# Attention on rounded f32 halves with scores and maxima on separate row halves, and a last layer norm done batch by batch

## The reference, cut to what matters

```python
# attention: x [4096, 256], 16 heads of D = 16, K = 64
qh, kh, vh = heads(q @ in_proj_weight.T + in_proj_bias);  qh = qh / sqrt(d)
scores = einsum('bhid,bhjd->bhij', qh, kh)
rel    = clip(pos[None, :] - pos[:, None], -K, K) + K
bias   = take_along_axis(einsum('bhid,rd->bhir', qh, rel_pe), rel, axis=-1)
attn   = softmax(scores + bias, axis=-1)
x = layernorm(x + einsum('bhij,bhjd->bhid', attn, vh) @ out_w.T + out_b)
# two layers on x seen as (2, 2048, 256), 8 heads of 64
for l in range(2):
    h = shift_token(x)
    q, k, v = split(h @ wqkv[l])          # l2 norm, scale, rotation
    x = x + local_attention(q, k, v) @ wo[l]          # windows of 128, one back
    h = layernorm(shift_token(x)) * lg + lb
    a, g = split(h @ w1[l] + b1[l])
    x = x + (a * gelu(g)) @ w2[l] + b2[l]
x = layernorm(x_before_the_layers + x)
```

## Time and profile before

| | |
|---|---|
| median of 3 runs | 5778.08 us (5756.49 to 5778.12) |
| the profiled execution's own time | 5783.44 us |
| its span | 5781.8 us |
| PE busy | 5294.7 us (92%) |
| DVE busy | 4105.4 us (71%) |
| ACT busy | 3109.6 us (54%) |
| POOL busy | 953.5 us (16%) |

### The profile page before, as it was taken

One profiled execution on the slowest core, in us unless ns is written; L12 is line 12 of the kernel. 1 busy time (PEld: TensorE's weight loads), 2 busy tenths in 40 slices (PEclk: granted clock), 3 DMA queues, 4 the chain that ended last, 5 costly groups with the idle time before them and its releaser, 6 DMA issues. The chain is left out here.

```text
span 5781.8 us, 113252 instructions
## 1 busy us (share of the span) xinstructions
PE 5294.7 (92%) x33984; PEld 2681.2 (46%) x33984; DVE 4105.4 (71%) x8598; ACT 3109.6 (54%) x4537; POOL 953.5 (16%) x704
## 2 busy tenths in 40 slices
PE   7499999999999999999999999985999898999895
PEld 3233333333333333333333333332888654888653
DVE  4388888888888888888888888832777433777434
ACT  3256666666666666666666666630555312565310
POOL 0111111111111111111111111101333101333100
PEclk8589999999999999999999999975999899999997
DMA  6511112111111111112111111112000000000000
GB/s 166 141 40 53 48 54 56 48 53 54 50 53 53 48 54 55 48 53 54 50 53 53 47 52 47 52 43 91 1 0 0 16 0 16 1 0 0 30 0 29
DMA packets 203462, 254.49 MB, mean 44 GB/s; under 512 B 71086, under 2 KB 132852, under 8 KB 201588
## 3 DMA queue, kind: packets, MB, share of 16 engines
q1 hardware_dynamic: 199524, 232.98, 14.3%
q0 software_dynamic: 3856, 20.45, 1.3%
HBM read 210.73 MB, written 42.47 MB: 44 GB/s over the span
## 5 line engine op out<-in xcount | busy, mean ns | idle before, releaser
L745 DVE TENSOR_REDUCE group_max<-shared_ps 128x1 f32<-128x512 f32 x4096 | 2684.7, 688 | 586.7 <-PE shared_ps L469 484.2
L622 ACT ACTIVATE probs<-scores 128x1024 f32<-128x1024 f32 x2048 | 2012.3, 1021 | 1052.9 <-PE scores L495 673.7
L469 PE MATMUL shared_ps<-keys,max_queries 96*128 96x512 bf16 x4096 | 1436.1, 385 | 3.2 <-issue 1.7
L495 PE MATMUL scores<-queries,keys 98*128 98x512 bf16 (+3 forms) x4096 | 1218.5, 372 | 86.6 <-ACT probs L622 85.6
L510 PE MATMUL out_ps<-probs,values 128*17 128x512 f32 x8192 | 1089.2, 604 | 0.4 <-ACT probs L622 0.4
L469 PEld LDWEIGHTS shared_ps<-keys,max_queries 96*128 96x128 bf16 x4096 | 396.1, 97 | 1123.5 <-DVE group_max L745 507.9
L215 POOL TENSOR_TENSOR near_window<-near_bias,one_f 128x1536 bf16<-128x1536 f32 x128 | 351.5, 2746 | 2953.7 <-DVE max_parts L739 2305.8
L495 PEld LDWEIGHTS scores<-queries,keys 98*128 98x128 bf16 x4096 | 360.3, 98 | 465.7 <-ACT probs L622 236.9
L1303 PE MATMUL quad<-h_T,w 128*128 128x512 f32 (+1 forms) x768 | 344.3, 599 | 1.9 <-ACT h_T L1417 1.9
L521 PE MATMUL shared_ps<-block_q,block_table 96*128 96x32 bf16 x4096 | 271.5, 233 | 65.2 <-POOL block_q L406 65.2
L521 PEld LDWEIGHTS shared_ps<-block_q,block_table 96*128 96x128 bf16 x4096 | 231.3, 114 | 171.8 <-issue 122.4
(11 more groups left out here) (186 smaller groups left out, 5639.0 us busy)
## 6 DMA issues: line engine op xcount, KB each, us to landing
keys<-k_parts SPq DMA_DIRECT2D x384, 96.0 KB, 2.1
values<-v_wide SPq DMA_DIRECT2D x128, 272.0 KB, 2.7
keys<-k_parts SPq DMA_DIRECT2D x384, 64.0 KB, 2.0
keys<-k_parts SPq DMA_DIRECT2D x128, 132.0 KB, 2.4
q_stack<-part SPq DMA_DIRECT2D x96, 128.0 KB
k_parts<-part SPq DMA_DIRECT2D x96, 128.0 KB
queries<-q_stack SPq DMA_DIRECT2D x128, 96.0 KB, 2.2
max_queries<-q_stack SPq DMA_DIRECT2D x128, 96.0 KB, 2.3
```

Source lines behind the costliest of these rows:

```text
L469: mm = pe.matmul(bank, max_queries[par][:, t * P:(t + 1) * P], keys[par][0:ROWS, (t + TPC * g) * P:(t + TPC * (g + 1)) * P], start=True, s ...
L495: mm = pe.matmul(out[:, 0:cut], keys[par][:, c * P:(c + 1) * P], queries[par][:, 0:cut], start=True, stop=True)
L622: act.activation(probs[s % 4][:], scores[s % 2][:], ACT.Exp).then_inc(exp_done, 1)
L745: dve.tensor_reduce(group_max[par][:, k:k + 1], bank, AX.X, ALU.max).then_inc(max_read, 1)
```

## The change

**Project.** Queries and keys are cut into two f32 numbers, `high` (rounded to F32R, PE's rounded f32 form) and `low` (the rest). Stored are `q_parts` and `k_parts` (high and low, once), `q_thirds` (three bf16 parts, for the bias alone), `edge_rows` (the two constant far biases per query, made by two more matmuls per chunk and stored with their low halves), and `v_wide` once per four chunks in pieces of 1088 bytes. A chunk has 18 stores instead of 26, and the buffers they read are doubled. The loop is unrolled.

**Attention.** The contraction has `KROWS` = 52 rows: two for the maximum, two for the far bias, and 48 for three products of halves. Keys of a whole head (`[P, N]`) are loaded once per head, twice into the same buffer: rows 0 to 51 serve the scores, rows 64 to 115 the maxima. Queries have the same two homes, and two versions of their far-bias rows (for keys to the left and to the right). Scores go to a ring of three single banks (`score_ps`), in which the bias, the rows of the maximum and the sum take their turns too; ACT does 32 exponentials of 512 columns. Maxima go to two pairs of banks (`max_ps`), one pair is reduced at once: 16 reductions of 128x1024. PE's turn is a `pv_quad`, then four times a bank of maxima and a score. A small POOL copy (`copy_max`) puts the maximum's rows into the second version of the queries.

```diff
+    ORDER = [5, 0, 1, 6, 2, 3, 7, 4] + list(range(8, TILES))
+    BIAS_TURN = {0: 0, 1: 1}
+    ROWS_TURN = 4
+    RING = 3
...
-        keys = [sb(f"keys{i}", [ROWS + MROWS, WIN_TILES * P], BF16) for i in range(2)]
-        queries = [sb(f"queries{i}", [ROWS + MROWS, CH], BF16) for i in range(2)]
-        max_queries = [sb(f"max_queries{i}", [ROWS, CH], BF16) for i in range(2)]
+        keys = [sb(f"keys{i}", [P, N], F32R) for i in range(2)]
+        queries = [sb(f"queries{i}", [P, 2, CH], F32R) for i in range(2)]
...
-        scores = [ps(f"scores{i}", [P, 2, CH]) for i in range(2)]
+        score_ps = [ps(f"score_ps{i}", [P, CH]) for i in range(RING)]
+        max_ps = [ps(f"max_ps{i}", [P, 2, CH]) for i in range(2)]
         out_ps = ps("out_ps", [P, CH])
-        shared_ps = [ps(f"shared_ps{i}", [P, CH]) for i in range(3)]
...
+            def max_pair(m, i, p, item):
...
+                        mm = pe.matmul(bank[:, a * P:z * P],
+                                       queries[par][P // 2:P // 2 + KROWS, side, t * P:(t + 1) * P],
+                                       keys[key_par][P // 2:P // 2 + KROWS, tile * P:(tile + z - a) * P],
+                                       start=True, stop=not inside)
...
+            def score(m, i, pos, bank):
...
+                        mm = pe.matmul(bank[:, a:z], keys[key_par][0:KROWS, tile % TILES * P:(tile % TILES + 1) * P],
+                                       queries[par][0:KROWS, side, a:z], start=True, stop=True)
...
+                def free(at):
+                    pe.wait_ge(score_read, items_before(m, i, at - 2))
+                    return score_ps[at % RING][:]
...
+            def exp_tile(m, i, pos, bank):
+                if ORDER[pos] in NEAR:
+                    act.wait_ge(near_added, at_step(m, i, len(NEAR), NEAR.index(ORDER[pos]) + 1))
+                act.wait_ge(pv_done, at_step(m, i, QUADS, pos // 4 + 1))
+                act.activation(probs[:, pos % 8, :], bank, ACT.Exp).then_inc(score_read, 1)
...
+            def pair_max(m, i, p, item, written):
+                t, j = p % TPC, p // TPC
+                dve.wait_ge(max_written, written)
+                dve.tensor_reduce(group_max[i % 2][:, t, j:j + 1], max_ps[item % 2][:], AX.XY, ALU.max
+                                  ).then_inc(max_read, 1)
```

```diff
-            for i in range(4):
-                sp.wait_ge(S.end_normed, (i + 1) * QUARTER)
...
+            for i in range(BATCHES):
+                sp.wait_ge(S.end_normed, i + 1)
...
+                    if ending and i < 2:
+                        (end_add, end_count)[i](past)
...
+                    if ending and i >= HT - 2:
+                        (end_params, end_norm)[i - (HT - 2)](past)
```

More of the change, by code:

```diff
@@ L371, in _ @@
+            with sp.Fori(0, LOOPED) as m:
+                for i in range(BODY):
+                    step(m, i, False)
+            for m in range(LOOPED, HEADS // 2):
+                for i in range(BODY):
+                    step(m, i, True)
         @block.gpsimd
@@ L526, in sum_quadrants @@
-            def sum_quadrants(n, par):
-                pe.wait_ge(out_copied, n + 2)
+                    pe.wait_ge(block_ready, at_step(m, e, 1, 1))
+                for k in range(UG):
+                    u = half * UG + k
+                    mm = pe.matmul(bank[:, k * TILES:(k + 1) * TILES],
+                                   block_table[b % 2][:, BLOCK_U - 1 - u:BLOCK_U - 1 - u + P],
+                                   block_q[b % 2][:, :, u], start=True, stop=True)
+                mm.then_inc(score_written, 1)
@@ L785, in _, with near_adds @@
-            chunk(TOTAL - 1, 1, 0)
+                dve.wait_ge(norm_step, at_step(m, i, 1, 1))
+                dve.tensor_tensor(attn[:, c * TPC:(c + 1) * TPC, bass.ds(h * D, D)], summed[:, :, 0:D],
+                                  inv_sum[:].to_broadcast([P, TPC, D]), ALU.mult).then_inc(max_read, 1)
+            def near_adds(m, i, last, turn, half):
+                n = m * BODY + i
+                for k in range(2):
+                    pos = 4 * (turn + 2) + 2 * half + k
+                    ahead, pos = pos // TILES, pos % TILES
+                    if ORDER[pos] in NEAR and (not last or n + ahead < TOTAL):
+                        at = STEP.index(("score", pos))
+                        near_add(*later(m, i, ahead), ORDER[pos], items_before(m, i, at) + 1, at)
@@ L1332, in _ @@
             pe.wait_ge(set_up, SET_UP)
-            with pe.Fori(0, DEPTH) as l:
+            for l in range(DEPTH):
                 pe.wait_ge(attn_w_in, l * 48 + 48)
@@ L1432, in _ @@
             act.wait_ge(set_up, SET_UP)
-            with act.Fori(0, DEPTH) as l:
+            for l in range(DEPTH):
                 act.preload_act_table(ACT.Exp)
@@ L1608, in _ @@
             dve.wait_ge(first_stored, 16)
-            with dve.Fori(0, DEPTH) as l:
+            for l in range(DEPTH):
                 dve.wait_ge(S.w_rounded, l + 1)
```

1092 lines of the change are left out of this document (601 added, 491 removed).

## The result

The changed kernel takes 7083.41 us (median of 4 runs, 6995.1 to 7173.99) against 5769.46. The ratio is 1.223, 95% interval 1.211 to 1.235; it is formed from the means of the fast runs, without the one of 7173.99, which is in the slower state. The forecast was 5739, in a range from 5520 to 5890.

A forecast was written before the change was run, and what follows sets the result against it. PE was taken to lead in attention. Attention +31, project -33, set-up +12 and end -49 make -39 on the profiled 5783.4, giving 5744; that execution lies 5 above the median, so 5739, range 5520 to 5890.

The forecast's parts named there:

- attention term: Attention: 119 chunks with bias at 0.25 us more and 8 without at 0.1 more, +31 us.
- The walk: Attention: PE's turns added up from durations in the earlier trace, 27.75 us per chunk against 27.5; chance 0.45.
- Halves side by side: Attention: score and maximum matmuls on the two row halves run at once, four pairs 0.95 us against 1.83.
- The rival that denied it: Attention: the halves run in series, 30.3 us per chunk and 6070 us total, 5900 if half as bad; chance 0.15.
- rule on loads: On PE: a weight load waits for the matmul before it; chance 0.03.
- The ring: Attention: a turn's fourth score waits for one of three banks, a loop of 1.27 us in a turn of 2.63.
- mode change: Attention, plain turn: PE's change of array mode, 0.09 us of the turn's 2.63.
- the ring costs less: Attention: hand-overs at the ring cost less than walked, 25.3 to 26.3 us per chunk, 5490 us total; chance 0.25.
- The POOL copy: Attention, before the next chunk's first score: taken at nothing, at most 1 us per chunk if late.
- The sign of the attention: Attention: slower than before, by 31 us.
- Project and set-up: Before the attention: project -33 us from 5.5 MB fewer stores, set-up +12 us from DVE's clearing of key buffers.
- End: After the layers' last batch: 11.6 us remain of 61, so -49 us.

The follow-up runs named there:

- e1: The changed kernel with the maxima reading queries from their own buffer and keys at row 0, so no two matmuls run side by side: 8950 us.
- e8: e4 plus v_wide stored once per four chunks in 1088-byte pieces, double-buffered bf16 parts and unrolled project loops: 5666.78 us, ratio 0.9821 to the kernel before.
- e4: The kernel before with only the layers and end of the changed kernel: 5716.87 us, ratio 0.9895.
- e3: The kernel before with scores and maxima cut to 52 rows and the exponential scaled by 0.001: 7502 us.
- e5: The kernel before with scores and maxima cut to 72 rows and the exponential scaled by 0.001: 5856 us.
- e6: The kernel before with scores and maxima cut to 64 rows and the exponential scaled by 0.001: 7178 us.
- e14: The kernel before with scores and maxima cut to 66 rows and the exponential scaled by 0.001: 6202 us.
- e7: The changed kernel with 12 rows of zeros added in each half, so scores and maxima use all 64 rows: 6218 us.
- e10: e7 with the two bias blocks behind turns 1 and 2 instead of 0 and 1: 6078 us.
- e2: The changed kernel with every matmul of the maxima over queries and keys issued twice into the same bank: 8167 us.
- e11: e7 with the four matmuls of maxima in turn 0 issued twice: 6482 us.
- e9: The changed kernel with each bias block in the chunks' loop issuing 1 matmul in place of 16: 6450 us.

## Why the prediction was wrong

**The step that failed** is the first number of its attention term. The walk turned waits and matmuls into microseconds with durations read at a clock of 0.99, and took that clock along into a kernel whose matmuls use 52 rows instead of 96. The clock fell to 0.65, and a chunk went from 27.75 us as walked to 38.33 as measured. Attention grew by 1389 us where 31 were forecast, an error of 1358; the other stages gave back 13 more than forecast. How much of the 1358 is the clock can be estimated from the chunks at full clock: 118 with bias at 28.35, seven without at 25.9, and some 42 us for the last two, which have few maxima or none left to make, are about 3570 us against the 4868 measured. So about 1300 us are the clock, and some 60 the walk itself. No rival held the clock, and neither did the range. The earlier trace rows has the clock stage by stage, 0.99 in the attention, and the prediction took it as a property of the stage, not of the matmuls in it.

**What stood in the rows.** The earlier trace rows has PE busy 97% at 0.99 in attention and 59% at 0.74 in the project stage. That looks as if the busy share decided. The changed kernel is busy 97% and gets 0.65, e1 99.5% and 0.51: busy time in a profile counts a matmul of 52 rows as fully as one of 128. The trace before could hardly show it, since its attention had no matmul of fewer than 96 rows, and the short groups of 64 rows in its layers stand in a stage with a mean of 0.96. What it did show, and the prediction passed over, are 12 falls at the sums.

**Halves side by side:** right, at full clock to 0.05 us a turn. The rival that denied it is refuted by the timeline. No run shows the "rule on loads" to which the forecast gives a chance of 0.03, a weight load that waits for the matmul before it; what the runs showed is that two scores are 0.23 apart when they queue (1693.98 to 1694.21 in the same trace), though the second needs new weights in the same rows: its load starts at 1694.03, beside the score before, and none shows between them. Only after the stall is the second pair 0.10 later (1693.64 to 1693.97). The sum for the turn is right by its total more than by its terms: its 0.95 is given as the price of four pairs, while in the trace the first three pairs lie within the loop of 1.27 (1693.64 to 1694.91), and it is the product with the values, 0.99, that takes that place.

**The ring:** right. In every plain turn at full clock the fourth score starts 1.19 to 1.29 us behind the first, 1.27 forecast. The 0.09 that the walk calls a mode change is in the traces as a time: before, 0.31 us pass from a turn's last maximum to the product, where queued matmuls are 0.22 apart, and in the changed kernel 0.33 from a pair to the near-window matmul behind it (1691.31 to 1691.64), where queued pairs are 0.23 apart. The other turns were sized too low: the walk erred by 0.6 us in a chunk, of which 0.2 lie in the turn of the first near-window matmuls alone (3.07 for 2.86), and the last two turns with the sum took 7.84 for 7.7. The rival "the ring costs less" is refuted. Two of the stated ranges don't follow from their own bounds: 26.8 and 28.05 a chunk give 5618 and 5777, not 5660 and 5810, and 25.3 to 26.3 a chunk are 150 to 280 us less than the 27.5 of before, not 60 to 310. The POOL copy, taken at nothing, did cost nothing: it was done at 1692.13, the next chunk's first score began at 1696.32.

**The sign of the attention at full clock** was right as well, its size was not: 28.35 against 27.49 with bias and 25.9 against 25.44 without are about 110 us, 31 were forecast. As an estimate, without any loss of clock the span would have been 7088 less about 1300, some 5790 us, against 5744 forecast on the same basis and 5782 before. So even then the changed attention would have given back all that the other stages bring, and the faster kernel that was forecast would probably not have come; the prediction's own mark against it, a chunk of 28.2 or more, is just passed at full clock too.

**Project and set-up:** -27 by the first sum, -21 forecast (-33 + 12). That the sum is near is partly luck: DVE begins the set-up at 184.1 us instead of 232.9 (-49), and from there to the first sum 133.9 us pass instead of 112.5 (+21). Nor were the bytes the whole reason: e8 gets 41 of the 49 us with the bytes of before. **End:** -56 in the trace and 59 us in the medians of e4, against -49: the stretch behind the last add is 9.6 us where 11.6 were forecast, and e4 has 64 us less behind the last sum. The rest lies within the layers, 5 us in the changed kernel and 14 in e4, but 5 again in e8, whose layers are those of e4; what made them shorter the runs don't say.

**What stays open:** e3, e5, e6 and e14 give the clock for each number of rows, not what sets it. Why it goes from 0.68 to 0.87 with two rows more than 64, while two halves at once (104 rows) get no more clock than 52 rows in series in the kernel before (0.63 to 0.65 and 0.65), was not settled; with 64 rows the two halves do get more, 0.87 (e7) against 0.68 (e6). Nor is the number of rows all: 52 rows in series have 0.65 in the kernel before and 0.51 in e1, which differ in number format (bf16 and f32), order and waits, and no run separates these.

## What to carry to other kernels

Before rewriting matmuls to contract over fewer rows, take the granted clock as an unknown of the sum: in a kernel bound by PE it was worth about 1300 us of 5770, more than any saving at stake. If a matmul's contraction is short, try padding it with rows of zeros (e7: 866 us less for no added instruction of PE, though not enough to win here). Stretches of tiny matmuls and waits that follow each other are worth breaking up as a trial (e10: 140 us by moving two blocks a turn, in one run each). Take a large change apart and keep the parts that leave the bound stage alone: e8 does, and is 1.8% faster than the kernel before (1.6 to 2.0%).

## What the runs showed of the hardware

- In the attention of the kernel before, TensorE's granted clock went with the rows that its matmuls of scores and maxima use, at a busy share of 97.6 to 98.8%: 0.65, 0.68, 0.87, 0.97, 0.99 for 52, 64, 66, 72 and 96 to 98 rows (e3, e6, e14, e5, before; one trace each).
- 12 rows of zeros added to the 52 of each half took the clock from 0.63 to 0.87 (changed kernel and e7, 400 to 3700 us, one trace each).
- Added matmuls of few rows did not raise it in two tries (e2 at 0.63, as the changed kernel; e11 at 0.81 against e7's 0.87).
- Most falls begin at the sum, 8 matmuls of 17 columns, which in the changed kernel stood behind waits of 0.32 and 0.55 us (1701.20, 1702.25): 113 of 115 in the changed kernel, 84 of 84 in e7, 92 of 108 in e10. Their mean length was 29.8, 12.9 and 5.5 us there, and 18.4 where the bias matmuls behind the sum were left out (e9).
- Two f32 matmuls on rows 0 to 51 and 64 to 115, writing different banks that ACT and DVE read in turn, start within 10 ns of each other (changed kernel, at 1693.64, 1693.97 and 1694.21) and each follow 0.23 from start to start for 512 columns, as the f32 matmuls of 128 rows do at 0.24.
